# A graph network layer: the receivers' one-hot rows of layer 1 written by ScalarE instead of VectorE

## What is computed

```
x_u = data @ var_u
x_v = data @ -var_u
logits = x_u[edge_src] + x_v[edge_dst] + var_c
q = jax.nn.softmax(logits, axis=-1)
x_sep = data[edge_dst] * edge_vals[:, None]
for m in range(8):
    agg = jax.ops.segment_sum(q[:, m:m + 1] * x_sep, edge_src, num_segments=num_v)
    y = y + agg @ var_w[m]
return y + var_b
```

## Time and profile before

| | |
|---|---|
| median of three runs | 2416.97 us (2416.3 to 2418.75) |
| profiled execution | 2419.39 us, its span 2417.6 us |
| VectorE busy in the span | 1317.0 us (54%) |
| GpSimd busy | 1680.1 us (69%) |
| TensorE matmul busy | 1718.0 us (71%) |
| ScalarE busy | 555.0 us (23%) |
| mean granted TensorE clock | 0.696 of full speed |

### The profile page before, as it was taken

The page is one execution under the profiler, slowest core; times in us unless marked ns, Lnnn a source line. Parts: engine busy times, 40 slices in busy tenths (PEclk is TensorE's granted clock), DMA queues, the critical chain, the costliest instruction groups (busy, mean ns, idle before and its releaser), DMA issues.

```text
span 2417.6 us, 50381 instructions
## 1 busy us (share of the span) xinstructions
PE 1718.0 (71%) x9991; PEld 1194.3 (49%) x9991; DVE 1317.0 (54%) x5192; ACT 555.0 (23%) x1977; POOL 1680.1 (69%) x1700
## 2 busy tenths in 40 slices
PE   4688889998888899898946555556556556556555
PEld 3355555555555555555534444445445444445444
DVE  5133332333322333322138888888888888888885
ACT  2233333333333333333111111111111111111110
POOL 2677777777777777777336777677777777777773
PEclk8798997989999988988655555555555555555555
DMA  3433333333333333333043333333333333333332
GB/s 73 98 70 68 69 68 69 71 68 71 68 68 69 69 67 71 69 68 68 20 77 94 91 94 92 90 94 93 90 94 92 91 94 92 92 93 93 90 94 60
DMA packets 269590, 191.00 MB, mean 79 GB/s; under 512 B 199089, under 2 KB 242640, under 8 KB 269566
## 3 DMA queue, kind: packets, MB, share of 16 engines
q0 software_dynamic: 66800, 113.26, 20.1%
q1 hardware_dynamic: 200822, 75.78, 13.4%
q10 hardware_dynamic: 1944, 1.69, 0.3%
HBM read 183.85 MB, written 6.69 MB: 79 GB/s over the span
## 4 chain that ended last, share of the span: by engine, by line
DVE 30%; issue 24%; PE 17%; DMA 11%; POOL 10%; DVEq 6%; ACT 1%; SPq 0%; ACTq 0%; POOLq 0%
POOL X L553 10%; DMA X<-table_src,slot_s 8%; DVE EQW L1103 4%; DVE EQW L1109 3%; PE bank L1325 3%; DVE OT L943 3%; PE bank L1308 3%; PE bank L1316 3%; PE bank L1334 2%; DVE EX L1149 2%; DVE r L1141 2%; DVE OE L1154 2%; DVE r L1136 2%; DVE r L1145 2%; DVEq L1168 2%
## 5 line engine op out<-in xcount | busy, mean ns | idle before, releaser
L561 POOL DMA_INDIRECT G<-table_node_and_list,slot_s x825 | 805.1, 976 | 362.2 <-issue 209.7
L553 POOL DMA_INDIRECT X<-table_src,slot_s x825 | 834.3, 1011 | 300.6 <-issue 264.9
L1443 PE MATMUL bank<-Q,G 125*64 125x128 f32 x1650 | 413.8, 422 | 181.7 <-DVE Q L1162 181.6
L957 DVE TENSOR_TENSOR sT<-sT,bank 65x16 f32 x275 | 46.2, 168 | 710.7 <-PE bank L1344 675.6
L1443 PEld LDWEIGHTS bank<-Q,G 125*64 125x64 f32 x1650 | 312.7, 221 | 194.6 <-issue 126.1
L1308 PE MATMUL bank<-filler 128*128 128x384 bf16 x1100 | 385.3, 350 | 2.2 <-issue 2.2
L1454 PE MATMUL bank<-R,w_z 65*64 65x64 f32 x1104 | 133.5, 315 | 270.0 <-DVE sT L1170 270.0
L943 DVE TENSOR_SCALAR OT<-KBT,base_p 48x375 bf16<-48x375 int32 x550 | 234.2, 426 | 92.7 <-DMA KBT<-in_dst 43.3
L1325 PE MATMUL bank<-XT,w_ex 128*64 128x375 f32 x550 | 263.9, 566 | 0.0
L1454 PEld LDWEIGHTS bank<-R,w_z 65*64 65x64 f32 x1104 | 122.5, 224 | 274.1 <-issue 274.1
L1316 PE MATMUL bank<-ident,X 125*128 125x125 f32 x825 | 151.8, 297 | 144.2 <-DMA X<-table_src,slot_s 114.4
(11 more groups left out here) (165 smaller groups left out, 1952.9 us busy)
## 6 DMA issues: line engine op xcount, KB each, us to landing
KBT<-in_dst SPq DMA_DIRECT2D x550, 70.3 KB, 2.1
X<-in_edge_attr SPq DMA_DIRECT2D x275, 93.8 KB
X<-table_src,slot_s POOLq DMA_INDIRECT x825
G<-table_node_and_list,slot_s POOLq DMA_INDIRECT x825
BW<-table_dst_parts SPq DMA_DIRECT2D x275, 6.0 KB
UW<-table_logit_src_parts SPq DMA_DIRECT2D x275, 0.8 KB, 1.6
table_node_and_list<-sm SPq DMA_DIRECT2D x1, 1562.5 KB
table_dst_parts<-G SPq DMA_DIRECT2D x1, 1171.9 KB
```

The source lines that it names most:

```text
L553: pool.indirect_dma_start(X[:, j, q, D:2 * D], None, tA, bass.IndirectOffsetOnAxis(ap=slot_s[:, j, q:q + 1], axis=0)).then_inc(gat_a[0][j] ...
L561: pool.indirect_dma_start(G[:, j, q, :], None, tH, bass.IndirectOffsetOnAxis(ap=slot_s[:, j, q:q + 1], axis=0)).then_inc(g_gather[j], 16)
L1443: last = pe.matmul(bank[2 + j % 2][0:D, 0:WM], G[0:P, j, q, 0:D], Q[:, j % 2, q].rearrange("p m n -> p (m n)"), start=(q == 0), stop=(q == ...
```

## The change

ScalarE writes the one-hot rows of layer 1 in two instructions. `window1_t` writes `OD = |base_p - KBT|` (48 x 375, f32), `window1_one` writes `OT = relu(1 - OD)`: one where receiver and node are equal, zero elsewhere, since both are whole numbers. Both are called for group g+1 in step g. ScalarE's step becomes: slots and `R` of g-2, `OD` and `OT` of g+1, the exponential of g-1; the exponential stood first before. `OD` has one buffer, and SyncE may load `KBT` again once `OD` of g-4 is written. VectorE no longer writes `OT` in layer 1. The rows of layer 0 (same function, L943 before) stay on VectorE.

```diff
--- before.py
+++ after.py
@@ -161,6 +161,8 @@
         H1 = sb("H1", [DC, RB, GE])
         H2 = sb("H2", [P, RB, TG, DC])
         KBT = sb("KBT", [WP, RB, GE], I32)
+        OD = sb("OD", [WP, GE])
+        one_col = sb("one_col", [WP, 1])
         OT = sb("OT", [WP, RB, GE], BF16)
         BW = sb("BW", [WP, RB, D], BF16)
         OE = sb("OE", [P, RB, TG, WG])
@@ -254,6 +256,7 @@
         u_OT, u_U, u_log, u_max, u_L, u_EX, u_EQ, u_EW, u_found, u_sum, u_den, u_rec, u_scale, u_head, u_OH = (
             sem(f"u_{n}") for n in ("OT", "U", "log", "max", "L", "EX", "EQ", "EW", "found", "sum", "den", "rec",
                                     "scale", "head", "OH"))
+        u_D = sem("u_D")
         u_Q, u_agg, u_R, u_y, u_acc = (sem(f"u_{n}") for n in ("Q", "agg", "R", "y", "acc"))
         slots_ready = [sem(f"slots_ready{l}") for l in range(2)]
         slots_g = sem("slots_g")
@@ -466,7 +469,7 @@
 
             def rows1w(t, j):
                 g = RB * t + j
-                done(sp, u_OT, t, j, RB)
+                done(sp, u_D, t, j, RB)
                 sp.sem_inc(sp_go, 1)
                 sp.dma_start(KBT[:, j, :], a["dst"][bass.ds(g * GE, GE)].partition_broadcast(WP)
                              ).then_inc(kbt_load[1][j], 16)
@@ -780,6 +783,17 @@
 
                 act.activation(EX[:, j], L[:, j], ACT.Exp).then_inc(u_EX, 1)
 
+            def window1_t(t, j):
+                act.wait_ge(kbt_load[1][j], (t + 1) * 16)
+                done(act, u_OT, t, j, 1)
+                act.activation(OD[:], KBT[:, j, :], ACT.Abs, bias=base_p[:, bass.ds(RB * t + j, 1)], scale=-1.0
+                               ).then_inc(u_D, 1)
+
+            def window1_one(t, j):
+                done(act, u_D, t, j)
+                done(act, u_U, t, j, RB)
+                act.activation(OT[:, j, :], OD[:], ACT.Relu, bias=one_col[:, 0:1], scale=-1.0).then_inc(u_OT, 1)
+
             def neighbours_w(t, j):
                 done(act, u_agg, t, j)
                 slots_w(1, t + 1, j)
@@ -788,11 +802,15 @@
                          ).then_inc(u_R, 1)
 
             def body1w(t, j):
+                back(neighbours_w, t, j, 2)
+                back(window1_t, t, j, -1)
+                back(window1_one, t, j, -1)
                 back(exps_w, t, j, 1)
-                back(neighbours_w, t, j, 2)
 
             for j in range(RB):
                 slots_w(1, 0, j)
+            window1_t(0, 0)
+            window1_one(0, 0)
             over_groups(act, body1w, DEPTH1)
 
             proof_ = load_proof(act)
@@ -845,6 +863,7 @@
                 step(dve.tensor_scalar(to, hs, 0.0, None, ALU.max))
 
             dve.memset(eps_col[:], EPS)
+            dve.memset(one_col[:], 1.0)
             dve.memset(no_key[:], -1.0)
             dve.memset(pairs[:], 0.0)
             win(dve.memset(ones[:], 1.0))
@@ -937,11 +956,11 @@
                 dve.tensor_copy(C[:, j], bank[6 + j % 2][0:P, 0:TG * DC].rearrange("p (q f) -> p q f", q=TG)
                                 ).then_inc(dve_g[0], 1)
 
-            def window_t(l, t, j):
-                dve.wait_ge(kbt_load[l][j], (t + 1) * 16)
-                done(dve, (f_h1, u_U)[l], t, j, RB)
+            def window_t(t, j):
+                dve.wait_ge(kbt_load[0][j], (t + 1) * 16)
+                done(dve, f_h1, t, j, RB)
                 dve.tensor_scalar(OT[:, j, :], KBT[:, j, :], base_p[:, bass.ds(RB * t + j, 1)], None,
-                                  ALU.is_equal).then_inc((f_OT, u_OT)[l], 1)
+                                  ALU.is_equal).then_inc(f_OT, 1)
 
             def window_e(t, j):
                 done(dve, f_seg, t, j, RB)
@@ -965,7 +984,7 @@
                 dve.tensor_reduce(pairs[:, bass.ds(t - 1, 1)], KQ, AX_X, ALU.add)
 
             def body0w(t, j):
-                back(lambda t, j: window_t(0, t, j), t, j, 0)
+                back(window_t, t, j, 0)
                 if not isinstance(t, int) and j == 1:
                     same_keys(t)
                 back(window_e, t, j, 2)
@@ -1179,7 +1198,6 @@
 
             def body1w(t, j):
 
-                back(lambda t, j: window_t(1, t, j), t, j, 0)
                 back(window_places, t, j, 2)
                 back(add_outputs, t, j, 2 * RB)
                 back(exp_sums, t, j, 2)
```

## The result

The changed kernel takes 2986.28 us (median of 4 runs, 2984.36 to 2991.77). Beside it the kernel before took 2416.8 us. The ratio is 1.236, with a 95% interval of 1.2346 to 1.2375: 23.6% slower, against 2970 us predicted. The profiled execution took 2984.36 us.

A forecast was written before the change was run, and what follows sets the result against it. VectorE was taken to bound layer 1 before the change. After it, 274 steps x 5.22 us plus 67 x 3.67 us make 1676.2 us instead of 1123.6 us, 552.6 us more: 2970 us, range 2860 to 3060 us.

The forecast's parts named there:

- the closed loop: Layer 1: the exponential behind the wait for the aggregate makes each group wait for the one before; 552.6 us more, 90%.
- Ordinary group: Layer 1, from Q to the next Q through four engines: 5.22 us a group, over 274 steps.
- The group with the outputs: Once a turn in layer 1, TensorE's outputs, waiting for VectorE's add, precede the aggregate: 3.67 us more, 67 times.
- VectorE's wait: Before L1151's sum, VectorE waits for the exponential: 1.6 us in an ordinary group, 5.3 us once a turn.
- The sum of all steps: Layer 1: ordinary steps and turns together take 1676.2 us instead of 1123.6 us, 552.6 us more.
- The price of an activation: ScalarE's two new instructions of 375 elements: 0.62 us each, with 0.473 us kept as the other end.
- What was said to cost nothing: Layer 1: loads of KBT are in time, and GpSimd's 3.85 us fits a 5.2 us step; no new wait.
- VectorE's relief would show: Rival at the sums of the exponential: it is not held up, GpSimd bounds at 3.85 us; 2343 us, 4%.
- the turn's term: Once a turn, Q to outputs 2.63 us and outputs to aggregate 1.73 us instead of 0.69 us: 3.67 us more.
- the outputs would hide: Rival: the turn's wait for the add is off the chain; 307 us more, 2724 us, 4%.
- Tables were not reloaded: Rival: ScalarE reloads its function tables in every group, two loads of 1.283 us; 703 us more, 3673 us, 1%.

The follow-up runs named there:

- e1_exp_first: The changed kernel with ScalarE's step reordered: exponential of g-1, OD and OT of g+1, slots and R of g-2; 2381.5 us, ratio 0.986 to before.
- e3_swap_only: The kernel before with only ScalarE's order swapped: slots and R of g-2, then the exponential of g-1, OT still on VectorE; 2699.3 us.
- e6_third_width: The changed kernel with both activations over 125 of the 375 columns, the rest of OT not written; 2869.3 us.
- e4_early_adds: The changed kernel with VectorE's add of the outputs one step earlier, group g-7 instead of g-8 in step g; 2737.1 us.
- e9_exp_first_add_behind_sums: e1_exp_first with VectorE's add and its register read moved behind the lists' sum in the step before; 2422.8 us, ratio 1.0047 to the kernel before.

## Why the prediction was right

**The place of the loss** was right: the closed loop, given 90%. e1_exp_first shows it from one side (same instructions, exponential free: the loss is gone), e3_swap_only from the other (order alone: half the loss).

**The terms.** Ordinary group: 5.22 us predicted, 5.33 us the mean of the three. Link by link in the group from 1811.41: Q to aggregate 0.62 us (0.69 predicted), aggregate to slots 1.68 (1.67), slots to R and R to OD 0.10 and 0.17 (0.10 and 0.15), OD to OT 0.71 (0.65), OT to exponential 0.52 (0.52), exponential to sum 0.24 (0.25), sum to Q 1.35 at the loop's turn. These rows show the link that was a little short, OD to OT:

```profile
1813.98 0.61 ACT L789 ACTIVATE OD<-KBT,base_p 48x375 f32<-48x375 int32 x1
1814.69 0.61 ACT L795 ACTIVATE OT<-OD,one_col 48x375 bf16<-48x375 f32 x1
```

0.10 us pass between OD's end and OT's start in three groups of four, and 0.02 us in the fourth; I had taken 0.03 us from an engine waiting for another. The group with the outputs: 8.91 us, 3.58 us more than the others, 3.67 predicted. Some of that agreement is luck. From Q by way of the outputs to the aggregate it took 4.50 us (1827.40 to 1831.90) and not 4.36: I had taken the full 0.33 us of OT off the way from Q to the outputs, which came out at 2.76 us and not 2.63. The links behind it were shorter in this group than in the others (aggregate to slots 1.62, OD to OT 0.63, sum to Q 1.14 us) and made up for it.

VectorE's wait was forecast at 1.6 us in an ordinary group and 5.3 us once a turn; the trace has 0.91 us at the loop's turn, 1.41, 1.48 and 5.15 us.

The sum of all steps was 552.6 us against 569.6 measured from Q to Q: 274 x 0.11 = 30 us too little for the ordinary groups, 67 x 0.09 = 6 us too much for the turns; the 7 us that are left go the other way, and I did not trace them. The median is 16 us above the forecast.

**The price of an activation** was the choice between two rows, the copy at 0.473 us and the square root with a bias from memory, which gave 0.63 and was taken at 0.62. Measured: 0.607 and 0.608 us. By the copy's row the forecast would have been 2890 us, 96 us short. The Trainium skill (ScalarE: Activation LUTs, Rules for kernel authors) gives about 0.3 us and 0.83 ns an element; e6_third_width agrees, with 0.30 us and 0.83 ns.

**What was said to cost nothing.** Of the loads of `KBT` and of GpSimd's gathers nothing shows in VectorE's waits after. GpSimd idles 927.3 us before its gathers instead of 362.2 us, and nobody waits.

**The rivals.** That VectorE's relief would show came true only when the order was undone, and then gave 2381.5 us, not 2343: GpSimd's 3.85 us a group was not reached. Here a step of the working failed. I had put the relief at OT's 0.33 us from start to start, as if what stood behind it would simply move up; a turn gained 0.14 us a group. In the forecast it stands only in the turn's term, as the 2.63 us from Q to the outputs: 0.13 us too little, 67 times, 9 us. In the ordinary groups VectorE waits anyway. That the outputs would hide was wrong by the 249 us that e4_early_adds gives back. Tables were not reloaded: the exponential's line has one load for 275 exponentials, the two activations take 0.61 us each, and the exponential starts before the second has ended.

```profile
L784 ACT ACTIVATE EX<-L x275: 205/206/222, 1262.9 to 2956.1; 125x24 f32<-125x24 f32 x138
L784 ACT ACT_TABLE_LOAD  x1: 1283/1283/1283, 1261.6 to 1261.6; - x1
```

The Trainium skill (ScalarE: Activation LUTs, Table sets: the hidden batching unit) has relu, abs and copy in every set; by that rule the same was to be expected, and the trace agrees.

## What to carry to other kernels

Before moving work to an idle engine, write down the loop that each wait in its list closes: what stands behind the wait, who needs it, and over how many groups the chain runs until it comes back. An instruction that others wait for belongs ahead of the wait for a later result, and new work belongs behind it but still ahead of the wait, if its own users are to get it in time. The order of e3_swap_only cost 283 us, and no busy share before it gives a warning: ScalarE was busy for 150.6 of the 1123.6 us of layer 1. The sign in the trace before was that once a turn TensorE waited 4.01 us for the add, and the exponential that then ran behind `R` was finished only 0.42 us before VectorE used it (1816.36 to 1816.78).

## What the runs showed of the hardware

- An activation with a bias from memory takes 0.61 us for 375 elements and 0.40 us for 125, whether it reads int32 and writes f32 or reads f32 and writes bf16 (0.607 and 0.608 us). A copy of 375 elements without a bias took 0.472 us; it read PSUM and had 128 partitions where the activations had 48.
- A register read from memory on VectorE took 0.30 us in its queue. In the chain of e9_exp_first_add_behind_sums 0.80 us pass from the first register instruction to the add (1815.25 to 1816.05), and no vector instruction starts in them. A vector instruction of 0.55 us ahead left VectorE idle for 0.37 to 0.51 us. Moving the add and its read there cost 41 to 45 us in one kernel and 64 us in another.
- An instruction of 0.41 us taken off the engine that sets the pace gave 0.14 us a group in e1_exp_first, a third of its length.
